# A graph layer with experts: an early expert order from seven token tiles, a list by matrix products, and maxima placed between attention units

## The chip, the core and the metric

The program runs on one core of a Trainium2 chip. The metric is device microseconds of one execution; of the kernel before, three runs gave a median of 1131.01 us (1125.94 to 1135.61). TensorE (PE) multiplies matrices into eight PSUM banks; VectorE (DVE), ScalarE (ACT) and GpSimd (POOL) compute; SyncE (SP) and POOL issue the DMAs. Each engine runs its own program in order, and they meet at semaphores.

## The reference

One layer on 1250 nodes of 768 channels, all float32. With `x` the input and `xn` its layer norm:

```
x = x + gnn(xn) + mix(xn)             # gnn holds its own norm, residual and Wu
gnn: out1 = gat(norm(xn), W1)  4 heads of 192;  out2 = gat(out1, W2)  2 heads of 96
     return concat(xn, out2) @ Wu + bu
gat: h = x @ W;  e = leaky_relu(s_src[src] + s_dst[dst], 0.2)
     ee = exp(e - max over the edges of dst);  out = sum(ee * h[src]) / sum(ee) + bias
mix: kqv = xn @ kqv_w.T + b;  linear attention over 12 heads with 32 features;  @ proj_w.T
x = x + ffn(layernorm(x))
ffn: probs = softmax(flat @ router_w.T)     # 8 experts
     top 2 of probs, each divided by 0.1 * sum of probs over all nodes + 0.91, then to sum 1
     out = sum over the two of gate * (silu(flat @ w1[e].T) @ w2[e].T)    # 768 -> 256 -> 768
```

The kernel turns the random edges into a dense table of counts, `cnt[src, dst]`.

## The kernel before

The nodes are ten **token tiles** (NT) of 128 rows, the last with 98. The five engine programs are written out by hand, and their order is the order of the work. PSUM banks are handed out in turn (`reserve`): `take` waits until the bank is free, `finished` until it is full, `evacuated` until it was copied.

**First half.** `x` is normalized and turned, keys, queries and mixing are multiplied in three-part float32 products, while VectorE and GpSimd build the table of counts. `u` (residual, mixture and the upper part of Wu) goes to `acc_d` in DRAM; `h1` is the product with W1 (20 steps, each half of a tile).

**Maxima.** For each destination tile, head and all sources, `masked_max` (L1337) subtracts a penalty (`pen`) from the row of scores (`a_row`) and takes the maximum. Tiles 0 to 3 are done for all heads at a time, then tiles 4 to 9 head by head. After each head `leaky_max` makes two columns, TensorE turns them (`mT`), VectorE copies them (L1375) and GpSimd writes them to `m_d` (L688). The rows `u1_row`, `u2_row` are read back broadcast to all partitions (L690, L695): head 0 behind the write of head 2, the others behind the last product of `h1`.

**Attention** (L1377, L991, L1896) goes through **units**: one head and one source tile. ScalarE makes `vbuf` (L1002), VectorE the score (`scores`, L1397), ScalarE the exponential (L1011), VectorE the product with `cnt` (L1408), TensorE ten matmuls (L1904) into five banks. There are three `pbuf` and two `vbuf`. The first attention has 40 units. Ahead of its first unit VectorE adds a bias row (L1451), and TensorE makes the small columns `b1T` (bias) and `csum` (sums of the router's columns), which VectorE takes behind the product of unit 0 (L1416 to L1420). Then come the product with W2, the same for two heads (`agg2`), and beside it products of `acc_d` with the router (`pre`).

**Routing.** When all `agg2` banks are copied (`rows_out_2`, L1438: five steps a bank), TensorE turns `o2` and multiplies each token tile with the lower part of Wu: two halves of 384 columns, and a separate pair of 8 columns for the router (`fin_step`, L1984). VectorE adds it to `x1` (`residual`, L1485), and SP stores `x1` into `out`. The tiles are routed in two `GROUPS`, 6 and 4: `shifted`, the softmax on ScalarE, `two_largest`; `ranks` on TensorE (prefix sums per expert, tile by tile) and `places` on VectorE. ScalarE normalizes `x1` into `yrow`, which SP stores into `y_d`, with the probabilities of the picks in its last 8 columns. GpSimd scatters each token's number to its place in `list_d` in DRAM (20 indirect DMAs, L724) and reads the list back. VectorE works out which expert each of the 27 **expert tiles** (NS) has, finds spare rows to fill the tiles (`matches`), and picks each tile's column out of the list (27 steps, L1612).

**Expert tiles.** For each, GpSimd fetches 128 rows of `y_d` (`fetch`, L733, three `xs` buffers), TensorE turns them, ScalarE and VectorE copy one half each into `xT` (L1111, L1645); then the first product (`first_product`, L2035), SiLU, a turn (`hT`), the second product, the gate, and GpSimd adds 128 rows into `out` by an indirect DMA (L751), each behind the end of the one before (L750).

## Time and profile before

| | |
|---|---|
| runs | 1131.01 us, median of 3 (1125.94 to 1135.61) |
| profiled execution | 1127.45 us; its span 1125.7 us |
| granted TensorE clock, mean | 0.905 |
| busy us: PE, PE's weight loads, DVE, ACT, POOL | 974.6, 831.3, 674.3, 417.4, 408.6 |
| first product of the first attention | starts 527.20 us |
| first fetch of an expert tile; first scatter | 922.21 us; 946.68 us |

### The profile page before, as it was taken

The page shows a single profiled execution, that of the slowest core. Times are in us where ns is not written, and L with a number is a line of the kernel's source. Part 1 is how long each engine was busy: PE and PEld are TensorE (multiplying, and loading weights), DVE is VectorE, ACT ScalarE, POOL GpSimd, SP SyncE. Part 2 cuts the span into 40 slices and gives each one's busy share as a digit, 9 for nine tenths or more (in the row PEclk, how much of TensorE's full clock was granted, in tenths as well). Part 3 has the DMA queues.
Part 4 walks back from the last instruction along what each step waited for, and adds up shares of the span by engine and source line. Part 5 has one row for each costly group of instructions (what it writes and reads, how often), then busy time and mean ns, then how long its engine had stood idle before and what let it go on. Part 6 is the DMA issues. An engine that isn't in the chain of part 4 may idle for free.

```text
span 1125.7 us, 14698 instructions
## 1 busy us (share of the span) xinstructions
PE 974.6 (87%) x5256; PEld 831.3 (74%) x5256; DVE 674.3 (60%) x1681; ACT 417.4 (37%) x658; POOL 408.6 (36%) x322
## 2 busy tenths in 40 slices
PE   3999988999999977964999989997789538999993
PEld 3898657776879977964999989896666436776772
DVE  7679997205643224678988868757957554333331
ACT  2544110333320003355788856438733302222220
POOL 3168888888888750003000000000000442344341
PEclk9999997899999988995999999868989558999997
DMA  9986456322544493114000000470054432656653
GB/s 294 220 202 161 78 114 168 62 24 1 113 65 76 84 266 132 25 43 177 13 15 1 1 1 1 154 269 13 1 177 173 138 129 50 133 115 121 129 119 56
DMA packets 77379, 115.77 MB, mean 103 GB/s; under 512 B 33089, under 2 KB 51899, under 8 KB 77309
## 3 DMA queue, kind: packets, MB, share of 16 engines
q0 software_dynamic: 36048, 40.48, 21.7%
q1 hardware_dynamic: 41261, 74.36, 20.4%
q8 instruction: 43, 0.70, 0.3%
q14 instruction: 27, 0.22, 0.1%
HBM read 85.18 MB, written 29.63 MB: 102 GB/s over the span
## 4 chain that ended last, share of the span: by engine, by line
PE 27%; DMA 15%; DVE 11%; issue 6%; ACT 3%; POOL 2%; another core or an unknown queue 1%; POOLq 0%; DVEq 0%; ACTq 0%
PE bank L1665 15%; DMA out<-yout,sb_negq 13%; PE bank L1904 9%; DVE pbuf L1408 3%; DVE pbuf L1397 3%; DVE sb_before L1342 2%; DMA cnt<-table 2%; PE bank L1676 1%; ACT h L988 1%; PE bank L1951 1%; ACT vbuf L1002 1%; POOL cnt L684 1%; DVE o L1443 1%; PE bank L1841 1%
## 5 line engine op out<-in xcount | busy, mean ns | idle before, releaser
L668 POOL DMA_INDIRECT table<-match_n,slot_ix x168 | 279.5, 1664 | 91.6 <-issue 47.2
L1904 PE MATMUL bank<-h,pbuf 128*128 128x193 f32 (+1 forms) x1200 | 189.8, 320 | 19.5 <-DVE pbuf L1408 18.9
L1904 PEld LDWEIGHTS bank<-h,pbuf 128*128 128x128 f32 x1200 | 182.9, 198 | 26.3 <-DVE pbuf L1408 23.7
L724 POOL DMA_INDIRECT list_d<-sb_wk,sb_negq x20 | 19.9, 993 | 331.9 <-DVE sb_negq L1561 326.4
L1342 DVE CUSTOM_DVE_ANT_0 sb_before<-a_row,pen 128x1280 bf16<-128x1280 f32 x60 | 89.4, 1491 | 18.7 <-ACT pen L945 12.5
L1206 DVE SCALAR_TENSOR_TENSOR junk_k<-keyrow,key,sb_before 128x384 uint8<-128x384 f32 x168 | 92.9, 615 | 9.1 <-DMA keyrow<-key_d 8.0
L1665 PE MATMUL bank<-xnT_hi,w_hi 128*128 128x512 f32 (+1 forms) x216 | 86.2, 399 | 10.6 <-issue 7.0
L1011 ACT ACTIVATE pbuf<-pbuf 128x1280 f32<-128x1280 f32 x60 | 76.7, 1278 | 42.4 <-DVE pbuf L1397 42.4
L1408 DVE SCALAR_TENSOR_TENSOR pbuf<-pbuf,cnt 128x1280 f32<-128x1280 f32 x60 | 88.8, 1487 | 0.0
L1665 PE MATMUL bank<-w_hi,xnT_hi 128*128 128x384 f32 x240 | 83.1, 346 | 0.0
L1665 PE MATMUL bank<-w_hi,xnT_lo 128*128 128x384 f32 x240 | 81.4, 339 | 0.0
L751 POOL DMA_INDIRECT out<-yout,sb_negq x27 | 42.9, 1589 | 105.8 <-DMA out<-yout,sb_negq 88.3
L1665 PE MATMUL bank<-w_lo,xnT_hi 128*128 128x384 f32 x240 | 81.3, 339 | 0.0
L1665 PE MATMUL bank<-w_all,xT 128*128 x324 | 76.8, 389 | 3.5 <-issue 3.5
L1665 PE MATMUL bank<-xnT_lo,w_hi 128*128 128x512 f32 (+1 forms) x216 | 79.4, 368 | 0.0
L1665 PE MATMUL bank<-xnT_hi,w_lo 128*128 128x512 f32 (+1 forms) x216 | 79.2, 366 | 0.0
L1665 PEld LDWEIGHTS bank<-w_all,xT 128*128 128x128 f32 x324 | 63.2, 196 | 18.3 <-issue 3.9
L1665 PE MATMUL bank<-w_all,hT 128*128 x216 | 74.8, 490 | 1.5 <-DVE hT L1652 1.5
L1397 DVE SCALAR_TENSOR_TENSOR pbuf<-u_row,sb_scol,vbuf 128x1280 f32<-128x1280 f32 x40 | 61.9, 1549 | 19.1 <-PE bank L1904 11.8
L833 ACT ACTIVATE kq<-bank,sb_kqb_c 128x512 f32<-128x512 f32 (+1 forms) x36 | 22.2, 618 | 123.3 <-PE bank L1665 103.2
L1665 PEld LDWEIGHTS bank<-xnT_hi,w_hi 128*128 128x128 f32 x216 | 42.2, 195 | 20.7 <-issue 14.5
L940 ACT ACTIVATE h<-bank,sb_rs 128x384 f32<-128x384 f32 x20 | 11.6, 582 | 122.3 <-PE bank L1665 122.3
(330 smaller groups left out, 1876.3 us busy)
## 6 DMA issues: line engine op xcount, KB each, us to landing
keyrow<-key_d SPq DMA_DIRECT2D x28, 384.0 KB
cnt<-table POOLq DMA_DIRECT2D x20, 320.0 KB, 8.9
w_all<-in_w1T SPq DMA_DIRECT2D x8, 768.0 KB
w_all<-in_w2T SPq DMA_DIRECT2D x8, 768.0 KB
u_row<-m_d POOLq DMA_DIRECT2D x8, 640.0 KB, 6.4
w_raw<-in_kqvT SPq DMA_DIRECT2D x4, 1152.0 KB, 16.9
y_d<-yrow SPq DMA_DIRECT2D x10, 388.0 KB
acc_d<-ubuf SPq DMA_DIRECT2D x20, 192.0 KB, 2.8
```

Source lines behind the costliest of these rows:

```text
L668: pool.indirect_dma_start(table[i], bass.IndirectOffsetOnAxis(ap=slot_ix[:, g:g + 1], axis=0), match_n[:, g:g + 1], None, compute_op=ALU.a ...
L724: pool.indirect_dma_start(list_d, bass.IndirectOffsetOnAxis(ap=place[0:n, k, t:t + 1], axis=0), token_no[0:n, t:t + 1], None, bounds_check ...
L751: pool.indirect_dma_start(out, bass.IndirectOffsetOnAxis(ap=sum_ix[:, s:s + 1], axis=0), yout[s % YO][:, :], None, compute_op=ALU.add, bou ...
L833: step(nc.scalar.activation(kq[j % 2][0][:, 0:w], b[:, 0:w], ACT.Identity, bias=kqb_c[:, col:col + 1]))
L940: nc.scalar.activation(h1[:, t, 2 * hf:2 * hf + 2, 0:C1], b[:, 0:HALF].rearrange("p (h c) -> p h c", h=2), ACT.Copy, scale=rs2[:, t:t + 1] ...
L1011: nc.scalar.activation(pbuf[i % 3][:, :], pbuf[i % 3][:, :], ACT.Exp).then_inc(e_done, 1)
L1206: nc.vector.scalar_tensor_tensor(out=junk_k[g % 2][:, :], in0=keyrow[c % KR][:, w:w + KW * P], scalar=key[:, g:g + 1], in1=before[:, first ...
L1342: ins = nc.vector.tensor_tensor_reduce(out=junk_m[:, :], in0=rows_a[h][:, :], in1=pen_t[:, :], scale=1.0, scalar=-3e38, op0=ALU.subtract, ...
L1397: nc.vector.scalar_tensor_tensor(out=pbuf[i % 3][:, :], in0=u1_r[h][:, :], scalar=scol[:, h, st:st + 1], in1=vbuf[i % 2][:, :], op0=ALU.ad ...
L1408: nc.vector.scalar_tensor_tensor(out=pbuf[i % 3][:, :], in0=pbuf[i % 3][:, :], scalar=2.0, in1=cnt[st][:, :], op0=ALU.min, op1=ALU.mult).t ...
L1665: return nc.tensor.matmul(o, l, r, start=first, stop=last)
L1904: ins = nc.tensor.matmul(b[:, d * stride:d * stride + chans + 1], score[:, dt * P:(dt + 1) * P], h_t[:, st, h, 0:chans + 1], start=st == 0 ...
```

## The change

**Expert order.** The groups are 7 and 3 tiles. From the first seven token tiles, which hold at least seven full expert tiles (NE), the first seven expert tiles are built and started: their rows are stored to a copy of their own (`early_d`) and fetched from there, while VectorE routes the last three. The other 20 wait for `y_d` and the late list. `x1` gets the 8 columns of probabilities and is normalized in place, after its store to `out`; `yrow` is gone, and there are four `xs`. For the early tiles ScalarE alone copies `xT`, `hT` and `y`.

**List.** The scatters to `list_d` are gone. For each pick two one-hot **marks** are made (row of the place; column times the token's number), and `listing` sums their products in a bank, 14 matmuls for the first group and 6 for the second, the latter between the first product of expert tile 2 and the turn of tile 1. `entries` picks the columns in two steps.

**Ranks and importance** are four and two matmuls wide in place of one or two for each tile. The router's 8 columns are merged into the first half of `wuo0` (392 columns), and `b2` is added by ScalarE when it copies `o2T`, so that `rows_out_2` has one product for five.

**Attention.** The maxima of heads 2 and 3 for tiles 4 to 9 stand behind twelve units of the first attention (`beside`), as do the bias row, the small columns and the rows of these heads. GpSimd writes heads 0 and 1 and reads their rows at once, before its table of numbers. ScalarE's ten steps on `cnt` (L975) stand in the last five tiles of `h1`. The core of the diff:

```diff
-        GROUPS = [range(6), range(6, NT)]
+        TABLE_W = E * KT
+        GA = 7
+        GROUPS = [range(GA), range(GA, NT)]
+        NE = -(-(2 * GA * P - E * (P - 1)) // P)
...
+                    r = slice(t * P, (t + 1) * P)
+                    if g == 0:
+                        sp.dma_start(early_d[r, :], x1[:, t, :]).then_inc(y_out[0], 16)
+                for t in tiles:
+                    r = slice(t * P, (t + 1) * P)
+                    sp.dma_start(y_d[r, :], x1[:, t, :]).then_inc(y_out[1], 16)
...
+
+            def rows_in_h(h):
                 pool.wait_ge(m_out[h], 16)
-            finished(pool, "h1", 1, NT - 1)
-            for h in range(1, H1):
                 pool.dma_start(u1_row[h][:, :], row_of(m_d, 2 * h)).then_inc(u_row_in[h], 16)
                 pool.dma_start(u2_row[h][:, :], row_of(m_d, 2 * h + 1)).then_inc(u_row_in[h], 16)
...
+            maxima_out(0), maxima_out(1)
+            finished(pool, "h1", 1, NT - 1)
+            rows_in_h(0), rows_in_h(1)
...
+            pool.wait_ge(y_out[0], 16 * GA)
             pool.wait_ge(rows_known, 1)
...
             for s in range(NS):
                 if s + XS < NS:
+                    if s + XS == NE:
+                        pool.wait_ge(y_out[1], 16 * NT)
+                        pool.wait_ge(rows_known, 2)
...
                 b = finished(act, "pen", dt, j)
                 nc.scalar.activation(pen[dt][:, 640 * j:640 * (j + 1)], b.bitcast(U16)[:, 0:640], ACT.Relu, scale=-BIG,
...
-                nc.scalar.activation(cnt[i][:, :], cnt[i][:, :], ACT.Identity, bias=less_c[:, 0:1]).then_inc(cnt_done, 1)
+                    if hf and t >= 5:
...
                 for t in GROUPS[g]:
-                    nc.scalar.activation(yrow[:, t, 0:D], x1[:, t, :], ACT.Identity, scale=rs2[:, t:t + 1],
+                    nc.scalar.activation(x1[:, t, 0:D], x1[:, t, 0:D], ACT.Identity, scale=rs2[:, t:t + 1],
                                          bias=shift[:, t:t + 1]).then_inc(y2_done, 1)
 
...
+                nc.vector.tensor_tensor(rw_raw[:, :, :], rw_raw[:, :, :], run[:, :].unsqueeze(1).broadcast_to([P, KD, E]),
+                                        ALU.add).then_inc(centred, 1)
+
+            beside = {3: (bias_row,), 6: (small_columns,), 9: (lambda: leaky_max_1(2),), 13: (lambda: maxima_rows(2),),
+                      21: (lambda: leaky_max_1(3),), 25: (lambda: maxima_rows(3),)}
+            for h, units in ((2, (1, 2, 4, 5, 7, 8)), (3, (10, 12, 14, 16, 18, 20))):
+                for dt, i in enumerate(units, 4):
+                    beside[i] = (lambda h=h, dt=dt: masked_max(pen[dt], a_row, (h,), dt),)
...
-                for d in range(5):
-                    ins = nc.vector.scalar_tensor_tensor(
-                        out=o2[:, 5 * i + d, h * C2:(h + 1) * C2], in0=pv[:, d, 0:C2], scalar=rec[:, d:d + 1],
-                        in1=b2_r[:, h * C2:(h + 1) * C2], op0=ALU.mult, op1=ALU.add)
-                    step(ins) if d < 4 else ins.then_inc(free("agg2", h, i), 1)
+                nc.vector.tensor_tensor(o2[:, 5 * i:5 * (i + 1), h * C2:(h + 1) * C2], pv[:, :, 0:C2],
+                                        rec[:, :].unsqueeze(2).broadcast_to([P, 5, C2]), ALU.mult).then_inc(free("agg2", h, i), 1)
...
+            def marks(g):
+
+                n = len(GROUPS[g])
+                for k in range(2):
+                    nc.vector.tensor_tensor(hot_row[:, k, 0:n, :], from_zero.unsqueeze(1).broadcast_to([P, n, P]),
+                                            chosen[g][:, k, 0, :].unsqueeze(2).broadcast_to([P, n, P]), ALU.is_equal)
+                    for i, t in enumerate(GROUPS[g]):
+                        ins = nc.vector.tensor_scalar(hot_col[:, k, i, :], columns, chosen[g][:, k, 1, i:i + 1],
+                                                      slot_no[:, t:t + 1], ALU.is_equal, ALU.mult)
+                    ins.then_inc(hot_done, 1)
...
+                hot = col_hot[:, 0:len(slots), :]
+                step(nc.vector.tensor_tensor(hot, columns.unsqueeze(1).broadcast_to([P, len(slots), TABLE_W]),
+                                             column[:, r].unsqueeze(2).broadcast_to([P, len(slots), TABLE_W]), ALU.is_equal))
...
+            def early_order():
+                step(nc.vector.tensor_tensor(filled[:, :, 0:NT - 1], n_early.unsqueeze(2).broadcast_to([P, E, NT - 1]),
+                                             steps_of.unsqueeze(1).broadcast_to([P, E, NT - 1]), ALU.is_ge))
+                step(nc.vector.tensor_reduce(out=n_full, in_=filled[:, :, 0:NT - 1], op=ALU.add, axis=AX.X))
+                tiles_before(n_full, first_early)
+                step(nc.vector.tensor_tensor(column_from, column_of, first_early, ALU.subtract))
+                in_order(EARLY_S, first_early, NE)
...
+            def entries(slots):
+                r, hot = slice(slots[0], slots[-1] + 1), col_hot[:, 0:len(slots), :]
+                step(nc.vector.tensor_tensor(hot, hot, listed.unsqueeze(1).broadcast_to([P, len(slots), TABLE_W]), ALU.mult))
+                step(nc.vector.tensor_reduce(out=row_f[:, r], in_=hot, op=ALU.add, axis=AX.X))
...
+            dve.wait_ge(pad_out, 16)
+            for t in GROUPS[0]:
+                residual(t)
+            inv_std_begin(mv3, span(0))
+            residual(GA)
+            shifted(0)
+            residual(GA + 1)
+            two_largest(0)
+            residual(GA + 2)
+            inv_std_begin(mv3, span(1))
+            places(0)
+            marks(0)
+            early_order()
+            b = finished(dve, "list", 0)
+            nc.vector.tensor_copy(listed, b[:, 0:TABLE_W]).then_inc(free("list", 0), 1)
+            evacuated(dve, "list", 0)
+            entries(EARLY_S)
+            nc.vector.tensor_scalar(token_ix[:, 0:NE], row_f[:, 0:NE], -1.0, None, ALU.add).then_inc(rows_known, 1)
+            shifted(1)
+            spare_places()
+            two_largest(1)
+            balances()
+            gates(0), gates(1)
+            places(1)
...
+            evacuated(dve, "spare")
+            marks(1)
+            gates(2), gates(3)
+            late_order()
+            b = finished(dve, "list", 1)
+            nc.vector.tensor_tensor(listed, listed, b[:, 0:TABLE_W], ALU.add).then_inc(free("list", 1), 1)
+            evacuated(dve, "list", 1)
+            entries(LATE_S)
+            r = slice(NE, NS)
...
-            b = take(pe, "csum")
-            for k in range(KD):
-                ins = mm(b[:, 0:E], ones[:, :], rw_raw[:, k, :], k == 0, k == KD - 1)
-            ins.then_inc(full("csum"), 1)
-            aggregate("agg", 0, H1, h1, S1, C1, 5, 2)
+                        if h * NT + st in behind:
+                            behind[h * NT + st]()
...
+            aggregate("agg", 0, H1, h1, S1, C1, 5, 2, {4: small_columns, 12: lambda: max_rows(2), 23: lambda: max_rows(3)})
...
-                        if hf == 0:
-                            evacuated(pe, "pre", len(PRE) - 1)
-                            for k in range(2):
-                                ins = mm(b[:, HALF:HALF + E], o2T[(t - 1) % 2][:, k, :], wuo_rw[:, k, :], k == 0, k == 1)
+                            w = wuo0[:, k, :] if hf == 0 else wuo[:, k, HALF:D]
+                            ins = mm(b[:, 0:w.shape[1]], o2T[(t - 1) % 2][:, k, :], w, k == 0, k == 1)
                         ins.then_inc(full("fin", t - 1, hf), 1)
...
+                of_group = slice(E * first, E * (first + n))
+                mm(b[:, 0:n * E], tri, row_t[:, 160:240][:, of_group], True, False)
+                mm(b[:, 0:n * E], ones[:, :], row_t[:, 240:320][:, of_group], False, True)
+                last = first + n - 1
+                mm(b[:, 64:64 + E], ones[:, :], seen[:, last, :], True, False)
+                mm(b[:, 64:64 + E], ones[0:rows(last), :], picks[0:rows(last), last, :], False, True).then_inc(full("rank", g), 1)
+
+            def listing(g):
+                b = take(pe, "list", g)
+                for k in range(2):
+                    pe.wait_ge(hot_done, 2 * g + k + 1)
+                    for i, t in enumerate(GROUPS[g]):
+                        n = rows(t)
+                        ins = mm(b[:, 0:TABLE_W], hot_row[0:n, k, i, :], hot_col[0:n, k, i, :], k == 0 and i == 0,
+                                 k == 1 and i == len(GROUPS[g]) - 1)
+                ins.then_inc(full("list", g), 1)
...
+            for t in range(NT + 1):
                 fin_step(t)
-            pe.wait_ge(numbers_done, 14)
+            pe.wait_ge(numbers_done, 12)
             ranks(0)
-            fin_step(NT)
-            ranks(1)
...
+                    if s + 1 == NE:
+                        pe.wait_ge(w_known, 2)
                     load_expert(s + 1)
                     first_product(s + 1)
+                if s == 0:
+                    spare_rows()
+                    ranks(1)
+                if s == 1:
+                    listing(1)
                 evacuated(pe, "h", s)
```

VectorE at the start of the first attention. Before:

```order
L1375 COPY sb_srow<-bank 20x128
L1451 TENSOR_TENSOR sb_row_b<-sb_row_b,sb_row_t 1x768
L1397 SCALAR_TENSOR_TENSOR pbuf_143<-u_row_133,sb_scol,vbuf_141 128x1280
L1397 SCALAR_TENSOR_TENSOR pbuf_144<-u_row_133,sb_scol,vbuf_142 128x1280
L1408 SCALAR_TENSOR_TENSOR pbuf_143<-pbuf_143,cnt_106 128x1280
L1416 COPY sb_b1T<-bank 96x8
L1418 TENSOR_SCALAR sb_run<-bank 128x8
L1420 TENSOR_TENSOR sb_rw_raw<-sb_rw_raw,sb_run 128x48
L1397 SCALAR_TENSOR_TENSOR pbuf_145<-u_row_133,sb_scol,vbuf_141 128x1280
L1408 SCALAR_TENSOR_TENSOR pbuf_144<-pbuf_144,cnt_107 128x1280
```

and now, where the names with `ISA` are a masked maximum and its read-out:

```order
L1405 COPY sb_srow<-bank 20x128
L1454 SCALAR_TENSOR_TENSOR pbuf_143<-u_row_133,sb_scol,vbuf_141 128x1280
L1454 SCALAR_TENSOR_TENSOR pbuf_144<-u_row_133,sb_scol,vbuf_142 128x1280
L1466 SCALAR_TENSOR_TENSOR pbuf_143<-pbuf_143,cnt_106 128x1280
L1454 SCALAR_TENSOR_TENSOR pbuf_145<-u_row_133,sb_scol,vbuf_141 128x1280
L1466 SCALAR_TENSOR_TENSOR pbuf_144<-pbuf_144,cnt_107 128x1280
L1374 ISA sb_before,sb_mxc<-a_row_119,pen_127 128x1280
L1374 ISA sb_mxc 128x1
L1454 SCALAR_TENSOR_TENSOR pbuf_143<-u_row_133,sb_scol,vbuf_142 128x1280
L1466 SCALAR_TENSOR_TENSOR pbuf_145<-pbuf_145,cnt_108 128x1280
```

The bias row is no longer ahead of the first score, the small columns are not behind the first product, and the first maximum of head 2 stands behind the product of unit 1.

TensorE between the last token tile and the first expert tile; `sb_row_t` with `sb_wq` or `sb_ones` are ranks, `sb_prob` the importance, `matches` the spare rows, `xs` the turned expert tiles. Before:

```order
L1665 MATMUL bank<-sb_row_t,sb_wq 128x8
L1665 MATMUL bank<-sb_row_t,sb_ones 128x8 x3
L1665 MATMUL bank<-sb_prob,sb_ones 128x8 x10
L1665 MATMUL bank<-sb_wq,matches 128x1 x8
L1676 MATMUL bank<-sb_ident,xs_171 128x128 x6
L1676 MATMUL bank<-sb_ident,xs_172 128x128 x6
L2045 TENSOR_LOAD sb_negq
L2045 ISA x2
L1665 ISA
```

and now, with the last token tiles at its head:

```order
L1770 MATMUL bank<-wuo,o2T_163 128x384 x2
L1770 MATMUL bank<-wuo_167,o2T_164 128x392 x2
L1770 MATMUL bank<-wuo,o2T_164 128x384 x2
L1770 MATMUL bank<-sb_row_t,sb_wq 128x56
L1770 MATMUL bank<-sb_row_t,sb_ones 128x56
L1770 MATMUL bank<-sb_row_t,sb_ones 128x8 x2
L1770 MATMUL bank<-hot_col,hot_row 128x80 x14
L1770 MATMUL bank<-sb_prob,sb_ones 128x72
L1770 MATMUL bank<-sb_prob,sb_ones 128x8
L2165 TENSOR_LOAD sb_negq
L2165 ISA x2
L1781 MATMUL bank<-sb_ident,xs_171 128x128 x6
L1781 MATMUL bank<-sb_ident,xs_172 128x128 x6
```

All token tiles are done before the ranks; those are four matmuls, the 14 list products follow, and the spare rows are gone from here. They stand with the ranks of the second group behind the first product of tile 1:

```order
L1770 MATMUL bank<-w_all,xT_181 128x256
L1770 MATMUL bank<-sb_wq,matches 128x1 x8
L1770 MATMUL bank<-sb_row_t,sb_wq 128x24
L1770 MATMUL bank<-sb_row_t,sb_ones 128x24
L1770 MATMUL bank<-sb_row_t,sb_ones 128x8 x2
L2186 MATMUL bank<-sb_ident,hs_176 128x128 x2
L1781 MATMUL bank<-sb_ident,xs_173 128x128 x6
```

so twelve small matmuls are new ahead of the turn (`hs`) of tile 0.

VectorE where the list comes in. Before, from the last step of the expert order:

```order
L1582 TENSOR_REDUCE sb_row_b<-sb_accb 128x27
L1597 CAST sb_negq<-sb_row_b 128x27
L1600 TENSOR_SCALAR matches<-sb_wq,sb_row_b 128x128 x8
L1604 TENSOR_SCALAR sb_run<-bank 128x8
L1606 TENSOR_SCALAR sb_run<-sb_run 128x8
L1607 RECIPROCAL sb_run<-sb_run 128x8
...
L1615 CAST sb_negq<-sb_row_t 128x3
L1612 SCALAR_TENSOR_TENSOR sb_row_b,sb_row_t<-sb_wq,sb_row_t,sb_negq 128x97 x24
L1615 CAST sb_negq<-sb_row_t 128x24
```

and now, for the first seven expert tiles:

```order
L1644 TENSOR_TENSOR col_hot<-sb_wq,sb_row_t 128x560
L1712 COPY sb_negq<-bank 128x80
L1670 TENSOR_TENSOR col_hot<-col_hot,sb_negq 128x560
L1671 TENSOR_REDUCE sb_row_t<-col_hot 128x7
L1715 TENSOR_SCALAR sb_negq<-sb_row_t 128x7
L1185 RECIPROCAL sb_rs<-sb_sq 128x3
L1186 TENSOR_TENSOR sb_r<-sb_rs 128x3
```

The 27 steps on the list are two large ones over seven tiles; the matches and the balances moved behind them.

## Rows read from the trace of the kernel before

**Rows 1.** The page: the chain that ended last, by line, share of the span.

```profile
PE bank L1665 15%; DMA out<-yout,sb_negq 13%; PE bank L1904 9%; DVE pbuf L1408 3%; DVE pbuf L1397 3%; DVE sb_before L1342 2%; DMA cnt<-table 2%; PE bank L1676 1%; ACT h L988 1%; PE bank L1951 1%; ACT vbuf L1002 1%; POOL cnt L684 1%; DVE o L
```

**Rows 2.** Timeline, VectorE, 493-522 us: start us, us, engine, line, operation, names, shapes, count.

```profile
493.70 1.49 DVE L1342 CUSTOM_DVE_ANT_0 sb_before<-a_row,pen 128x1280 bf16<-128x1280 f32 x1
...
495.24 1.49 DVE L1342 CUSTOM_DVE_ANT_0 sb_before<-a_row,pen 128x1280 bf16<-128x1280 f32 x1
...
520.97 0.94 DVE L1451 TENSOR_TENSOR sb_row_b<-sb_row_b,sb_row_t 1x768 f32<-1x768 f32 x1
```

**Rows 3.** Timeline, GpSimd and ScalarE, 500-520 us; in brackets the idle time before, and its releaser.

```profile
500.30 0.53 POOL L688 DMA_DIRECT2D m_d<-sb_srow  x1 [10.24 <-DVE sb_srow L1375]
...
511.42 0.55 POOL L690 DMA_DIRECT2D u_row<-m_d  x1
...
517.37 2.61 ACT L1002 ACTIVATE vbuf<-u_row,sb_a 128x1280 f32<-128x1280 f32 x2 [5.99 <-DMA u_row<-m_d]
```

**Rows 4.** DMA issues, 496 to 535 us: count, KB each, median us to landing.

```profile
w2g_raw<-in_W SPq DMA_DIRECT2D x1, 576.0 KB, 5.1
```

**Rows 5.** Timeline, TensorE, 517-533 us; and one row of the chain, us of six units.

```profile
527.20 6.05 PE L1904 MATMUL bank<-h,pbuf 128*128 128x193 f32 x20
...
608.71 19.98 PE bank L1904 x120
```

**Rows 6.** Timeline, VectorE, 572-576 us: first two units back to back.

```profile
572.63 1.48 DVE L1408 SCALAR_TENSOR_TENSOR pbuf<-pbuf,cnt 128x1280 f32<-128x1280 f32 x1
...
575.49 1.48 DVE L1408 SCALAR_TENSOR_TENSOR pbuf<-pbuf,cnt 128x1280 f32<-128x1280 f32 x1
```

**Rows 7.** Windows of 4 us: length, busy us by engine, granted clock, DMA share, GB/s.

```profile
796.00:800.00 4.00, 3.22 (x27) 2.89 (x26) 4.00 (x4) 3.66 (x4) 0.00 (x0) 1.00 0.00 0
...
812.00:816.00 4.00, 2.16 (x12) 1.92 (x12) 3.95 (x4) 2.05 (x2) 0.00 (x0) 0.53 0.00 0
...
896.00:900.00 4.00, 3.31 (x16) 3.32 (x16) 0.53 (x4) 0.00 (x0) 3.08 (x4) 0.50 1.03 381
```

**Rows 8.** Timeline, TensorE, 836-943 us.

```profile
836.22 1.06 PE L1676 MATMUL bank<-sb_ident,o 128*96 128x128 f32 x4 [3.14 <-DVE o L1443]
...
849.71 0.51 PE L1665 MATMUL bank<-sb_row_b,o2T 96*128 96x8 f32 x4
...
850.07 1.54 PE L1665 MATMUL bank<-wuo,o2T 96*128 96x384 f32 x4
...
853.32 1.54 PE L1665 MATMUL bank<-wuo,o2T 96*128 96x384 f32 x4
...
876.01 0.57 PE L1665 MATMUL bank<-sb_row_t,sb_wq 128*128 128x8 f32 x2 [4.91 <-issue]
...
876.43 0.57 PE L1665 MATMUL bank<-sb_row_t,sb_ones 128*128 128x8 f32 x2
...
933.40 7.97 PE L1665 MATMUL bank<-w_all,xT 128*128 x24 [3.51 <-issue]
```

**Rows 9.** Timeline, VectorE, 870-934 us.

```profile
870.98 0.20 DVE L1512 TENSOR_REDUCE sb_r<-sb_prob 128x6 f32<-128x48 f32 x1
...
881.31 0.17 DVE L1546 TENSOR_SCALAR sb_row_b<-sb_row_t 128x8 f32<-128x8 f32 x1 [5.40 <-PE bank L1665]
...
881.78 0.61 DVE L1549 TENSOR_TENSOR sb_accb<-bank,sb_wq 128x432 f32<-128x432 f32 x1
...
920.03 0.32 DVE L1612 SCALAR_TENSOR_TENSOR sb_row_b<-sb_wq,sb_row_t,sb_negq 128x97 f32<-128x97 f32 x1 [8.25 <-DMA sb_negq<-list_d]
...
932.65 1.02 DVE L1645 COPY xT<-bank 128x384 f32<-128x384 f32 x2
```

**Rows 10.** Timeline, GpSimd, 922-1117 us.

```profile
922.21 1.06 POOL L734 DMA_INDIRECT xs<-y_d,sb_negq  x1 [3.80 <-DVE sb_negq L1615]
...
946.68 1.65 POOL L751 DMA_INDIRECT out<-yout,sb_negq  x1 [9.77 <-DVE yout L1659]
...
1115.49 1.55 POOL L751 DMA_INDIRECT out<-yout,sb_negq  x1 [4.67 <-DMA out<-yout,sb_negq]
```

470 lines of the change are left out of this document (245 added, 225 removed).

## The prediction

> **What bounds the kernel now.** I read the chain of waits first, then the windows, then the timeline of each engine at the places that the change touches. By line the chain is matrix products of the first half (15%), the scatters into `out` (13%) and the attention products (9%) [rows 1]. Three stretches matter.
>
> *Before and in the first attention.* VectorE makes the masked maxima at 1.54 us each [rows 2], six a head for four heads, until 520.8; TensorE stands still. The u rows of head 0 are fetched only behind the maxima of head 2: issued at 511.42, used by ScalarE at 517.37, so 5.95 us [rows 3]. TensorE begins at 527.20, at half clock (6.05 us for the first unit), and then takes 19.98 / 6 = 3.33 us a unit [rows 5]. VectorE needs 575.49 - 572.63 = 2.86 us a unit [rows 6]: TensorE bounds, and VectorE has 0.47 us to spare in each unit.
>
> *Routing.* The second attention's products end 3.14 us before 836.22, at 833.1; the restart runs at half clock, then a token tile takes 853.32 - 850.07 = 3.25 us [rows 8]. VectorE then routes in two groups, waits 5.40 us for the first ranks and 8.25 us for the list that goes through DRAM [rows 9]; the first token rows are fetched at 922.21 and the first scatter starts at 946.68 [rows 10].
>
> *Expert tiles.* 27 scatters, each behind the one before: (1115.49 - 946.68) / 26 = 6.49 us [rows 10]. The end is the first scatter plus a fixed 26 x 6.49.
>
> **The attention.** The u rows of head 0 can now be asked for right behind the maxima of head 1, at 500.30 + 0.6 = 500.9 [rows 3]; they would be there at 506.9, but share the DMA engines with the load of W2, which takes 5.1 us to land [rows 4], and that of Wu. Bounds: 506.9 (no sharing) and 506.9 + 5.1 = 512.0 (all of it); I take 508.5, nearer to the first, since those loads start earlier. Leak 1.3 (half of 2.61 [rows 3]), two scores of 1.5 and a product of 1.4 (a pair is 2.86 [rows 6]) put the first matmul at 514.2, 13.0 us earlier than 527.20. The bias row (0.94 [rows 2]) and the 5 us of small columns between VectorE and TensorE are no longer ahead of it; they go behind units 3 to 6.
>
> But VectorE now carries twelve maxima in units 1 to 20. Until product 20 is made: 20 pairs x 2.86 = 57.2, 12 x 1.54 = 18.5, bias row, small columns, one leaky maximum and one row copy 2.7; so 514.2 + 78.4 = 592.6, plus 3.33 for its matmuls: 595.9. Before, TensorE had unit 20 done at 527.20 + 6.05 + 20 x 3.33 = 599.9. A head's change costs both about 1.4 by ScalarE's bank copies, and some 1.5 more where VectorE is the one that is late; the second leaky maximum adds 0.8. Left: 4.0 - 2.3 = 1.7; I take **-1 us**. The gain is lost since VectorE, which has the rows of head 1 copied by 500.3 [rows 3], stands idle until the u rows are there, and pays the maxima later, when it has 0.47 us a unit to hide them. Bounds: -4 and +5 (landing at its two ends, and the waits at the heads' change doubled).
>
> The move of ten subtractions on ScalarE into the last tiles of h1 costs nothing: they are hidden by the h1 products, and done by 502, before the u rows; uncovered they would hold product 0 (12 us in one piece before). Head 2's rows are ready by unit 17 and needed at 19.
>
> **Routing, as a table of times** (profile's clock, attention left out):
> - Second attention's end: one product of 480 elements in place of five steps, and TensorE asks for the first bank alone. Transposes start at 833.1 instead of 836.2: -3.1. Without the idle 3.14 us the clock should stay at its upper level (I assume it).
> - A token tile: 3.25 less 850.07 - 849.71 = 0.36 for the eight-column matmuls [rows 8], plus 0.03: 2.9. Ten tiles in a row: 834.3 + 29 = 863.3; the seventh at 854.6, its sums and statistics on VectorE 2 us later, 856.6.
> - A residual is two sums and two statistics passes over 384 elements, 0.5 each by the 0.61 for 432, and two small steps of 0.2: 2.5. The top two of six tiles took from 870.98 to 881.31 - 5.40 = 875.9, so 5.5 for seven [rows 9]. Residual 7 with one step more, shifts (nine small steps), residual 8, top two: 2.7 + 1.9 + 2.5 + 5.5, so 869.2. Ranks are four matmuls in place of twelve; one takes 876.43 - 876.01 = 0.43 us at half clock [rows 8], done at 871.1, hidden by residual 9 (2.5 us, to 871.7). The wait of 5.40 is gone.
> - Places: two steps of 504 elements at 0.7 (by 0.61 for 432) and ten small ones of 0.23: 3.7. Marks: per pick 896 elements, by the same row 1.1 us (bounds 0.9 and 1.3), and seven of 80 elements at some 0.18 (0.17 for 8, 0.32 for 97 [rows 9]): 2 x 2.3 = 4.6. Order of seven tiles: some 16 small steps of 0.2 to 0.3 and one of 560 elements: 4.2. To 884.2. The 14 list matmuls (0.43 each, 6 us) overlap with the last two and are done at 884. List, entries, indices: 0.3 + 2 x 0.75 + 0.2: **886.1**.
> - Stores: two weight loads (1.57 MB) and seven tiles (2.78 MB) from 871.5 at 381 GB/s [rows 7] are 11.4 us: 883 to 884, so no wait, if they are served in order.
> - Fetch at 886.3 against 922.21: **-35.9**.
> - Fetch to scatter: 24.5 us before. The 3.51 us idle ahead of the first product [rows 8], which ended when VectorE, busy with the list until then, had copied xT at 932.65 + 1.02 [rows 9], is gone, since ScalarE copies: -3.5. The fetch flies beside the second copies of the stores: +1.5 (0 to +5). Twelve small matmuls (spare rows, ranks of group 1) now stand before the first hT: 2.7 at full clock, 5.2 at half: +2.7. The second half of y is copied behind the first: +0.6. Gates: shifts, matches, top two, balances and two gates (some 10 us of small steps) end about 896, ahead of the first y at 909.7. Sum +1.3, taken down to +0.7 for the longer cover of the evacuations.
> - First scatter: 946.7 - 35.9 + 0.7 = **911.5**, -35.2.
> - Six list matmuls between first products cost tile 1 some 1.3; TensorE has about 0.3 a tile to spare: **+1**.
> - Late list: VectorE waits for ranks at 905.7, then places 2, marks 2.1, gates 2, order 6.5, entries 2 x 1.75 and rest: 923.5. GpSimd wants it behind scatter 2, at 925; TensorE needs those rows at 936. Hidden; if late beyond some 8 us, each us counts.
>
> Sum against the profiled execution: 1127.45 - 35.2 + 1 - 1 = 1092.3. The median shown, 1131.01, is 3.6 above it; I take about half of that: **1094 us**.
>
> At one point a rule speaks against the change. In the windows VectorE paces TensorE at 796 to 800 with 3.22 of 4 us busy, and the clock is full; at 812 to 816 with 2.16 busy it is 0.53 [rows 7]. In the new attention TensorE would be busy 3.33 of 4.4 us, so 3.0 of 4, between the two. The Trainium skill (TensorE: Matmul & The Clock Gate, "A second HAM failure mode: psum-queue depth-cycling") says that frequent short idle times between groups of matmuls can make the clock swing. By the row the sum is the one above; by that rule it is rival C.
>
> **Rivals.**
> - A, the first fetch is held by the stores. If the second copies (2.78 MB more) are served with the first ones, all seven land at 871.5 + 7.13 MB / 381 GB/s = 890.2 instead of 884, 4 us behind the list, and the fetch may take 4 more: 1102. For it: the DMA share is 1.03 while such stores run [rows 7]. The Trainium skill (DMA: Bandwidth & Descriptors, "Issuing engines are not separate DMA queues") says that issues of different engines interleave on the same engines, which is this rival's ground. Against: the stores stand in one queue in the right order.
> - B, VectorE's attention stretch is longer: waits of the kind at the heads' change recur in each unit with a maximum, 0.8 us x 12: 1104.
> - C, slower: half clock through units 0 to 25. A unit then takes 6.05: 514.2 + 26 x 6.05 = 671.5 against 527.2 + 6.05 + 25 x 3.33 + 1.4 = 617.9, +54 in place of -1: 1149. It decides only if 17 or more of 26 units run so, as 2.72 a unit has to eat 34 us and 11 more. Against it: at half clock a unit fills VectorE's 4.4 us wholly, TensorE has no idle left, and it came back from such a state in the first attention within two units.
> - D, the early tiles start no earlier than some 895 and B holds as well, or C for a third of the units: 1120, within 1%.
>
> **How the numbers follow.** Forecast 0.68, A 0.14, B 0.10, C 0.04, D 0.04. Its own range is 1087 to 1101 by the bounds above. To leave out C and D and little else the range is 1084 to 1111. A measurement here can tell about 1%, 11 us: faster 0.92, same 0.04, slower 0.04.
>
> **What would show it.** Right: first matmul of the first attention near 514, its last about where it was; transposes at 833 with a full clock; first fetch near 886, first scatter near 911, 6.5 us steps, no wait of TensorE for tile 7. Wrong: a u row used after 512; granted clock under 0.9 in units 1 to 20; the fetch released by a store; a gap ahead of scatter 7.

## The result, and the profile after

The changed kernel takes 1093.36 us, the median of four runs (1085.47 to 1098.63), against 1131.63 us (1125.94 to 1135.61) of the kernel before: a ratio of 0.967, 95% interval 0.963 to 0.971. Two later comparisons gave 0.971 (0.967 to 0.975) and 0.965 (0.962 to 0.969). The profiled execution took 1085.47 us, span 1083.7, granted clock 0.933: it is the fastest of the four, 6.8 us under the sum of the forecast, while the median lies 1 us above that sum.

The page's chain by line, as [rows 1] (L1770 and L2008 are the helpers' lines that were L1665 and L1904):

```profile
PE bank L1770 15%; DMA out<-yout,sb_negq 13%; PE bank L2008 6%; DVE pbuf L1466 5%; DVE pbuf L1454 4%; DMA cnt<-table 3%; PE bank L1781 1%; ACT vbuf L1025 1%; DMA early_d<-x 1%; ACT h L1011 1%; DVE sb_before L1374 1%; PE bank L2061 1%; DMA u_row<-m_d 1%; DMA xs<-early_d,sb_negq 1%; POOL cnt L707 1%
```

The scatters' share is the 13% that it was. New in the chain is `early_d<-x`, the stores of the early tiles.

**First attention.** VectorE, start and length, as [rows 2]: its copy of head 1's rows, the first scores, and two of head 3's maxima behind units.

```profile
502.38 0.28 DVE L1405 COPY sb_srow<-bank 20x128 f32<-20x128 f32 x1 [0.37 <-PE bank L1937]
...
512.95 3.01 DVE L1454 SCALAR_TENSOR_TENSOR pbuf<-u_row,sb_scol,vbuf 128x1280 f32<-128x1280 f32 x2 [10.28 <-ACT vbuf L1025]
...
575.52 1.47 DVE L1374 CUSTOM_DVE_ANT_0 sb_before<-a_row,pen 128x1280 bf16<-128x1280 f32 x1
...
582.66 1.47 DVE L1374 CUSTOM_DVE_ANT_0 sb_before<-a_row,pen 128x1280 bf16<-128x1280 f32 x1
```

TensorE in the same places, as [rows 5]:

```profile
517.41 12.48 PE L2008 MATMUL bank<-h,pbuf 128*128 128x193 f32 x60 [15.07 <-DVE pbuf L1466]
...
572.60 6.80 PE L2008 MATMUL bank<-h,pbuf 128*128 128x193 f32 x40 [0.63 <-DVE pbuf L1466]
...
579.92 6.80 PE L2008 MATMUL bank<-h,pbuf 128*128 128x193 f32 x40 [0.52 <-DVE pbuf L1466]
```

The first product comes 15.0 us behind the copy of head 1's rows (27.7 before). The first u rows are used at 511.47, 9.1 us behind that copy. From 575.52 on VectorE repeats every 7.14 us (582.66 - 575.52): two units of 2.86 and a masked maximum. TensorE stands idle 0.52 to 0.63 us ahead of each such pair and is no longer the bound. One window over this stretch shows what the clock did (columns as in [rows 7]):

```profile
530.00:610.00 80.00, 72.30 (x433) 68.07 (x433) 75.67 (x85) 56.20 (x61) 1.66 (x3) 1.00 0.05 18
```

TensorE busy 72.30 of 80 us, clock 1.00 throughout.

**Second attention.** VectorE's copies of two finished banks stand between units; the first of them, before (five steps), and the wait for TensorE that follows:

```profile
805.74 1.73 DVE L1443 SCALAR_TENSOR_TENSOR o<-bank,sb_rec,sb_accb 128x96 f32<-128x96 f32 x5
...
819.64 1.55 DVE L1397 SCALAR_TENSOR_TENSOR pbuf<-u_row_b,sb_scol,vbuf 128x1280 f32<-128x1280 f32 x1 [1.46 <-PE bank L1904]
```

and after (one step), with a window over the stretch that follows it:

```profile
802.26 0.66 DVE L1494 TENSOR_TENSOR o<-bank,sb_rec 128x480 f32<-128x480 f32 x1
```

```profile
804.00:808.00 4.00, 2.69 (x24) 2.52 (x24) 3.93 (x5) 2.75 (x3) 0.00 (x0) 1.00 0.00 0
```

From 796 to 820, cut in windows of 4 us, this is the least that TensorE is busy in the changed kernel (2.69 of 4), and the clock is 1.00 in all of them. Before, it was busy 1.61 of 4 us at 808 to 812, and the clock of the next window is 0.53 [rows 7].

**Routing.** TensorE, as [rows 8]:

```profile
825.82 0.61 PE L1781 MATMUL bank<-sb_ident,o 128*96 128x128 f32 x4
...
826.92 2.88 PE L1770 MATMUL bank<-wuo,o2T 96*128 96x392 f32 x8 [0.49 <-ACT o2T L1103]
...
829.85 2.77 PE L1770 MATMUL bank<-wuo,o2T 96*128 96x392 f32 x8
...
861.38 0.65 PE L1770 MATMUL bank<-sb_row_t,sb_wq 128*128 128x56 f32 x2 [6.16 <-issue]
...
886.77 2.82 PE L1781 MATMUL bank<-sb_ident,xs 128*128 128x128 f32 x12 [2.95 <-DMA xs<-early_d,sb_negq]
```

The first transposes overlap the last products of the attention (3.14 us idle before); a token tile takes 829.85 - 826.92 = 2.93 and then 2.83 us. The ranks begin at 861.38 and are eight records in place of 24. VectorE, as [rows 9], in the first group: ranks read, places, a mark of 896 elements, and the row numbers handed to GpSimd:

```profile
863.82 0.17 DVE L1590 COPY sb_row_b<-bank 128x8 f32<-128x8 f32 x1
...
864.70 0.68 DVE L1596 TENSOR_TENSOR sb_accb<-bank,sb_wq 128x504 f32<-128x504 f32 x1
...
867.47 1.09 DVE L1613 TENSOR_TENSOR hot_row<-sb_wq,sb_row_b 128x896 f32<-128x896 f32 x1
...
878.52 0.17 DVE L1715 TENSOR_SCALAR sb_negq<-sb_row_t 128x7 uint32<-128x7 f32 x1
```

The rank row has no idle time in brackets: the wait of 5.40 us is gone. The last row ends the early list at 878.7. GpSimd, as [rows 10]: first fetch, scatters 0 and 1, the fetch of tile 7 (the first from `y_d`), last scatter:

```profile
879.71 1.13 POOL L747 DMA_INDIRECT xs<-early_d,sb_negq  x1 [244.63 <-DMA early_d<-x]
...
904.79 1.64 POOL L771 DMA_INDIRECT out<-yout,sb_negq  x1 [14.54 <-DVE sb_row_b L1695]
...
912.22 2.39 POOL L771 DMA_INDIRECT out<-yout,sb_negq  x1 [4.40 <-ACT yout L1160]
...
921.12 1.06 POOL L747 DMA_INDIRECT xs<-y_d,sb_negq  x1 [0.30 <-issue]
...
1074.50 1.56 POOL L771 DMA_INDIRECT out<-yout,sb_negq  x1 [4.75 <-DMA out<-yout,sb_negq]
```

The first fetch names an early store as its releaser, but it starts 1.0 us behind the end of the list, and in the repeat a0 below, where the list is named, it is 0.95: the stores ended at about the time of the list. TensorE uses the fetched rows at 886.77, 7.06 us after the issue. Before it was 4.03, from 922.21 [rows 10] to this row:

```profile
926.24 1.54 PE L1676 MATMUL bank<-sb_ident,xs 128*128 128x128 f32 x6 [11.34 <-DMA xs<-y_d,sb_negq]
```

The fetch of tile 7 had no wait.

Here is the way from one profiled execution to the other, cut at events that both have:

| stretch | before | after | difference | forecast |
|---|---|---|---|---|
| start to the copy of head 1's rows | 499.46 | 502.38 | +2.9 | 0 |
| to the last product of the first attention | 167.03 | 165.52 | -1.5 | -1 |
| to the first product of the second | 102.87 | 97.97 | -4.9 | 0 |
| to its last product | 63.73 | 60.04 | -3.7 | 0 |
| to the first transposes | 3.13 | -0.09 | -3.2 | -3.1 |
| to the first fetch | 85.99 | 53.89 | -32.1 | -32.8 |
| to the first scatter | 24.47 | 25.08 | +0.6 | +0.7 |
| to the last scatter | 168.81 | 169.71 | +0.9 | +1 |
| to the end | 10.21 | 9.20 | -1.0 | 0 |
| sum | | | -42.0 | -35.2 |

### The profile page after: what moved, and what is told of

Its sections match the earlier page's. It is cut to its first block, busy times and chain, and to the rows that moved or that the text cites. A ratio compares the mean times of both kernels' runs of the same rounds, so it can differ in the third digit from the quotient of the medians.

```text
span 1083.7 us, 14577 instructions
## 1 busy us (share of the span) xinstructions
PE 947.0 (87%) x5216; PEld 809.1 (75%) x5216; DVE 667.2 (62%) x1635; ACT 427.8 (39%) x689; POOL 386.6 (36%) x298
## 4 chain that ended last, share of the span: by engine, by line
PE 23%; DMA 18%; DVE 12%; issue 6%; ACT 3%; POOL 1%; SPq 0%; POOLq 0%; DVEq 0%; ACTq 0%
PE bank L1770 15%; DMA out<-yout,sb_negq 13%; PE bank L2008 6%; DVE pbuf L1466 5%; DVE pbuf L1454 4%; DMA cnt<-table 3%; PE bank L1781 1%; ACT vbuf L1025 1%; DMA early_d<-x 1%; ACT h L1011 1%; DVE sb_before L1374 1%; PE bank L2061 1%; DMA u_row<-m_d 1%; DMA xs<-early_d,sb_negq 1%; POOL cnt L707 1%
## 5 line engine op out<-in xcount | busy, mean ns | idle before, releaser
L2008 PE MATMUL bank<-h,pbuf 128*128 128x193 f32 (+1 forms) x1200 | 189.9, 318 | 38.8 <-DVE pbuf L1466 35.8
L2008 PEld LDWEIGHTS bank<-h,pbuf 128*128 128x128 f32 x1200 | 180.7, 195 | 47.7 <-DVE pbuf L1466 43.4
L747 POOL DMA_INDIRECT xs<-early_d,sb_negq x7 | 7.4, 1058 | 250.5 <-DMA early_d<-x 244.6
L1770 PE MATMUL bank<-xnT_hi,w_hi 128*128 128x512 f32 (+1 forms) x216 | 85.4, 395 | 12.6 <-issue 9.0
L1770 PE MATMUL bank<-w_hi,xnT_hi 128*128 128x384 f32 x240 | 83.9, 350 | 0.0
L1770 PE MATMUL bank<-w_hi,xnT_lo 128*128 128x384 f32 x240 | 82.3, 343 | 0.0
L1770 PE MATMUL bank<-w_lo,xnT_hi 128*128 128x384 f32 x240 | 82.1, 342 | 0.0
L1770 PE MATMUL bank<-xnT_lo,w_hi 128*128 128x512 f32 (+1 forms) x216 | 78.8, 365 | 0.0
L1770 PE MATMUL bank<-xnT_hi,w_lo 128*128 128x512 f32 (+1 forms) x216 | 78.3, 363 | 0.0
L1770 PE MATMUL bank<-w_all,hT 128*128 x216 | 76.7, 498 | 1.5 <-DVE hT L1755 1.5
L1770 PE MATMUL bank<-w_all,xT 128*128 x324 | 74.9, 382 | 0.0
L1770 PEld LDWEIGHTS bank<-w_all,xT 128*128 128x128 f32 x324 | 62.1, 192 | 13.9
L1770 PEld LDWEIGHTS bank<-w_all,hT 128*128 128x128 f32 x216 | 39.2, 191 | 27.3 <-issue 3.3
L1770 PEld LDWEIGHTS bank<-xnT_hi,w_hi 128*128 128x128 f32 x216 | 41.8, 193 | 22.5 <-issue 16.5
```

The lines of the kernel that those rows point to most:

```text
L1770: return nc.tensor.matmul(o, l, r, start=first, stop=last)
L2008: ins = nc.tensor.matmul(b[:, d * stride:d * stride + chans + 1], score[:, dt * P:(dt + 1) * P], h_t[:, st, h, 0:chans + 1], start=st == 0 ...
```

## Experiments

All changes are to the changed kernel, and all ratios are to the kernel before, measured beside it. Two runs repeat the changed kernel as a base. Times of one kernel spread by up to 1.5%, so most verdicts rest on stretches of the trace, each from one profiled execution.

**The changed kernel again.**

> The changed kernel again, as the base of the others. Theory T1 (the forecast's working held; the profiled execution came 6.8 us below the sum because TensorE's clock was granted fully in two stretches that the change does not touch): ratio to the kernel before 0.965 to 0.969, and in this profile the first fetch comes 53 to 55 us after the end of the second attention's products, the first scatter 25 us after the fetch, the other 26 scatters 6.5 us apart, while the time from the first attention's last product to the second's last is anywhere between 158 and 167 us. Rival T2 (the change itself shortened that middle stretch): it is 158 us again, within 1 us.

Ratio 0.9711 (0.9673 to 0.9749), a little above the range expected. From transposes to fetch 53.83 us, fetch to scatter 24.84, the other 26 scatters 6.66 apart and not 6.5: 173.1 us from the first to the last, where the kernel before took 168.8 and the first profile of the changed one 169.7. In the twelve profiles of the changed kernel and its variants it is 169.7 to 173.1; of the kernel before there is one. The middle stretch, from the last product of the first attention to the last of the second, took 162.9: T2 falls, but T1 holds in half only. Cut in two, the second attention is 60.04 us here too, as in all profiles of kernels with the one-step copy, so that part belongs to the change. The stretch between the attentions is what varies. The same 656 to 658 products, in the kernel before, in the changed one, and in e9 below, one window each:

```profile
666.49:769.36 102.87, 90.43 (x658) 89.45 (x657) 68.39 (x215) 52.71 (x153) 0.00 (x0) 0.81 0.36 120
```

```profile
667.90:765.87 97.97, 85.54 (x656) 84.56 (x656) 68.36 (x215) 52.48 (x153) 0.00 (x0) 0.85 0.38 129
```

```profile
658.49:767.81 109.32, 96.88 (x658) 95.83 (x657) 68.37 (x215) 52.91 (x153) 0.00 (x0) 0.76 0.35 115
```

Their length goes with the granted clock: 0.81, 0.85, 0.76 for 102.87, 97.97, 109.32 us. In this repeat it was 102.87, as in the kernel before.

> The changed kernel once more, beside e10_fill_hold on the same chip: ratio to the kernel before 0.966 to 0.971. In its profile the second attention takes 60.0 us, and from the end of its products to the first fetch 53.8, as in the two before; the stretch between the attentions takes anything from 98 to 109 us, in steps that go with half clock.

Ratio 0.9652 (0.9618 to 0.9686), just below the range expected. Second attention 60.04, then 53.99 from the transposes to the first fetch, the stretch between the attentions 101.24; the first and the last scatter 172.8 apart.

**The maxima ahead of the attention.**

```diff
-            beside = {3: (bias_row,), 6: (small_columns,), 9: (lambda: leaky_max_1(2),), 13: (lambda: maxima_rows(2),),
-                      21: (lambda: leaky_max_1(3),), 25: (lambda: maxima_rows(3),)}
-            for h, units in ((2, (1, 2, 4, 5, 7, 8)), (3, (10, 12, 14, 16, 18, 20))):
-                for dt, i in enumerate(units, 4):
-                    beside[i] = (lambda h=h, dt=dt: masked_max(pen[dt], a_row, (h,), dt),)
+            beside = {3: (bias_row,), 6: (small_columns,), 13: (lambda: maxima_rows(2),), 25: (lambda: maxima_rows(3),)}
+            for h in (2, 3):
+                for dt in range(4, NT):
+                    masked_max(pen[dt], a_row, (h,), dt)
+                leaky_max_1(h)
```

> All twelve maxima of heads 2 and 3 stand ahead of the first attention again, where VectorE waits for the u rows; everything else as changed. T1 (placing them beside the units was worth about nothing, since the gain ahead is paid back in the units): the first product starts near 527 instead of 517, units take 3.33 us each, the last product ends 667 +- 2 as with the change; time within 0.3% of the changed kernel. Rival T3 (the placement carries part of the gain): the last product ends 8 to 13 us later and the time is 0.7 to 1.2% above the changed kernel.

The last product came at 672.99, with head 1's rows copied at 502.05: 170.9 us between them, against 165.5, 166.8 and 165.5 in the three profiles of the changed kernel. So 4 to 5 us worse, between T1 and T3. TensorE at the start, and a window over the stretch where the last two rows begin:

```profile
526.64 15.83 PE L2008 MATMUL bank<-h,pbuf 128*128 128x193 f32 x80 [24.63 <-DVE pbuf L1466]
...
546.12 1.51 PE L1770 MATMUL bank<-sb_ones,sb_row_b 1*96 1x1 f32 x16
...
547.90 2.02 PE L1770 MATMUL bank<-sb_rw_raw,sb_ones 128*128 128x8 f32 x12
...
549.78 30.04 PE L2008 MATMUL bank<-h,pbuf 128*128 128x193 f32 x160
```

```profile
547.00:560.00 13.00, 13.00 (x69) 12.91 (x69) 6.16 (x8) 4.78 (x4) 0.00 (x0) 0.74 0.00 0
```

TensorE bounds the units here, and the small columns between units 4 and 5 take 3.7 us of it (3.2 in the changed kernel). Behind them eight units take 30.04 us and not 8 x 3.33 = 26.6, since the clock of 547 to 560 is 0.74: 3.4 us. Such a stretch need not belong to the edit. Behind the same small columns, e10 below ran 540 to 550 at a clock of 0.66 and e2, with the same attention code, at 1.00. Without these 3.4 us e1 would stand at 167.5, 1 to 2 us above the changed kernel, which T1 allows. So the run speaks against T3; it doesn't show that the placement beside the units is worth anything. In time this kernel was at 0.9648 (0.9603 to 0.9693), no slower than the changed one measured beside it (0.9711), with intervals that overlap.

**Maxima of head 2 in the wait for the u rows.**

```diff
-            beside = {3: (bias_row,), 6: (small_columns,), 9: (lambda: leaky_max_1(2),), 13: (lambda: maxima_rows(2),),
+            beside = {3: (bias_row,), 6: (small_columns,), 13: (lambda: maxima_rows(2),),
                       21: (lambda: leaky_max_1(3),), 25: (lambda: maxima_rows(3),)}
-            for h, units in ((2, (1, 2, 4, 5, 7, 8)), (3, (10, 12, 14, 16, 18, 20))):
-                for dt, i in enumerate(units, 4):
-                    beside[i] = (lambda h=h, dt=dt: masked_max(pen[dt], a_row, (h,), dt),)
+            for dt in range(4, NT):
+                masked_max(pen[dt], a_row, (2,), dt)
+            leaky_max_1(2)
+            for dt, i in enumerate((1, 5, 8, 12, 15, 19), 4):
+                beside[i] = (lambda dt=dt: masked_max(pen[dt], a_row, (3,), dt),)
```

> Six maxima of head 2 stand in the 10.3 us in which VectorE waits for the u rows; those of head 3 stand behind units 1, 5, 8, 12, 15 and 19. T1: VectorE's 0.47 us to spare in a unit then hides one maximum in three to four units, TensorE bounds all units: start at 517, 6.0 + 39 x 3.33 + 3 x 1.4 = 140, so the last product ends at 657 to 660 instead of 667.9, and the time is 8 to 10 us (0.7 to 0.9%) below the changed kernel. Rival T4 (the units are paced by waits of the three score buffers, not by VectorE's sum): at most 2 us are gained.

Ratio 0.9604 (0.9574 to 0.9633), 1.0% under the changed kernel measured beside it, so 11 us, of which the attention in the trace shows 5 to 6.5. Start of the products to their end 144.9 us, so 160.25 from the copy of head 1's rows, 5.2 to 6.5 less than with the change. T4 falls. T1's 140 was too short: it left out the small columns (3.2 us), and each maximum still costs TensorE a pause:

```profile
552.69 13.67 PE L2010 MATMUL bank<-h,pbuf 128*128 128x193 f32 x80 [0.74 <-DVE pbuf L1468]
...
567.11 10.12 PE L2010 MATMUL bank<-h,pbuf 128*128 128x193 f32 x60 [0.63 <-DVE pbuf L1468]
...
577.97 13.38 PE L2010 MATMUL bank<-h,pbuf 128*128 128x193 f32 x80 [0.74 <-DVE pbuf L1468]
...
592.09 10.80 PE L2010 MATMUL bank<-h,pbuf 128*128 128x193 f32 x60 [0.74 <-DVE pbuf L1468]
```

0.63 to 0.74 us stand ahead of each restart. In the group of four units from 577.97 to 592.09 VectorE's sum is the smaller one (4 x 2.86 + 1.49 = 12.93 against 4 x 3.33 = 13.32), and the pause is there all the same.

**Bias row and small columns in that wait too.**

```diff
-            beside = {3: (bias_row,), 6: (small_columns,), 9: (lambda: leaky_max_1(2),), 13: (lambda: maxima_rows(2),),
+            beside = {2: (lambda: masked_max(pen[9], a_row, (2,), 9), lambda: leaky_max_1(2)), 13: (lambda: maxima_rows(2),),
...
+            bias_row()
+            for dt in range(4, NT - 1):
+                masked_max(pen[dt], a_row, (2,), dt)
+            small_columns()
+            for dt, i in enumerate((5, 8, 11, 14, 17, 20), 4):
+                beside[i] = (lambda dt=dt: masked_max(pen[dt], a_row, (3,), dt),)
...
-            aggregate("agg", 0, H1, h1, S1, C1, 5, 2, {4: small_columns, 12: lambda: max_rows(2), 23: lambda: max_rows(3)})
+            small_columns()
+            aggregate("agg", 0, H1, h1, S1, C1, 5, 2, {12: lambda: max_rows(2), 23: lambda: max_rows(3)})
```

> As e2_fill, and the bias row and the small columns stand ahead of the first attention too, in the wait for the u rows; the sixth maximum of head 2 stands behind unit 2 and those of head 3 behind units 5, 8, 11, 14, 17 and 20. T1 (TensorE bounds the units once VectorE's maxima are hidden, so what it does between units counts in full): the 3.5 us of small columns between units 4 and 5 are gone, and from VectorE's copy of head 1's rows to the last product of the attention it takes 156 to 157.5 us, where e2_fill took 160.25 and the changed kernel 165.5 to 166.8. Rival T8 (the small columns ahead push the first product later by as much): 160 us again.

160.21 us, as T8 said, but not for its reason: the first product came no later (15.29 us behind the copy). The columns were done by 502.4, and then:

```profile
499.62 2.73 PE L1773 MATMUL bank<-sb_rw_raw,sb_ones 128*128 128x8 f32 x12
...
510.53 11.64 PE L2011 MATMUL bank<-h,pbuf 128*128 128x193 f32 x60 [8.17 <-DVE pbuf L1469]
...
523.73 10.11 PE L2011 MATMUL bank<-h,pbuf 128*128 128x193 f32 x60 [1.56 <-DVE pbuf L1469]
...
534.59 10.12 PE L2011 MATMUL bank<-h,pbuf 128*128 128x193 f32 x60 [0.74 <-DVE pbuf L1469]
```

With a maximum in every third unit, three units take 10.86 us, while TensorE's sum is 9.99 and VectorE's 10.07 (3 x 2.86 + 1.49): the pauses (1.56, then 0.74 each), now seven maxima beside units and not six, ate what the columns gave back. Ratio 0.962 (0.959 to 0.966).

**Five steps for a bank of the second attention.**

```diff
-                nc.vector.tensor_tensor(o2[:, 5 * i:5 * (i + 1), h * C2:(h + 1) * C2], pv[:, :, 0:C2],
-                                        rec[:, :].unsqueeze(2).broadcast_to([P, 5, C2]), ALU.mult).then_inc(free("agg2", h, i), 1)
+                for d in range(5):
+                    ins = nc.vector.scalar_tensor_tensor(
+                        out=o2[:, 5 * i + d, h * C2:(h + 1) * C2], in0=pv[:, d, 0:C2], scalar=rec[:, d:d + 1],
+                        in1=ones[:, 0:C2], op0=ALU.mult, op1=ALU.mult)
+                    step(ins) if d < 4 else ins.then_inc(free("agg2", h, i), 1)
```

> The copy of each bank of the second attention is five steps of VectorE again (0.35 us each, the multiplier of ones in the place of b2) instead of one of 0.66 us. Theory T6 (a term the forecast left out: two of the four copies stand between units of the second attention, which VectorE bounds, and the longer ones leave TensorE idle until its clock is halved): from the first to the last product of the second attention 63.7 us instead of 60.04, and 1 us more ahead of the transposes behind it; 4 to 5 us in all. Rival T7 (the copies beside units cost only their own length): 60.04 + 2 x 1.07 = 62.2, and 1 more behind, so 3.2 us in all.

The second attention took 64.64 us and 0.98 more until the transposes: 5.7 us in all, T6's mechanism at a somewhat larger size; T7's 62.2 falls. Of the 4.6 us within the attention about 2.1 are the longer copies themselves (2 x 1.07). VectorE, and then two windows over the same place (columns as in [rows 7]):

```profile
811.82 1.73 DVE L1495 SCALAR_TENSOR_TENSOR o<-bank,sb_rec,sb_ones 128x96 f32<-128x96 f32 x5
...
826.08 1.55 DVE L1454 SCALAR_TENSOR_TENSOR pbuf<-u_row_b,sb_scol,vbuf 128x1280 f32<-128x1280 f32 x1 [1.81 <-PE bank L2011]
```

```profile
812.00:818.00 6.00, 3.61 (x32) 3.45 (x32) 5.68 (x12) 4.31 (x4) 0.00 (x0) 1.00 0.00 0
...
818.00:824.00 6.00, 4.32 (x22) 4.08 (x22) 5.93 (x6) 3.63 (x3) 0.00 (x0) 0.51 0.00 0
```

TensorE is busy 3.61 of 6 us while VectorE makes the steps, the granted clock falls to 0.51 in the next window, and only then VectorE waits for TensorE (1.81 us). With the one-step copy, in the changed kernel above, neither happens. The ratio was 0.9669 (0.9627 to 0.9711); 5 us are 0.5%, which the times here don't resolve.

**No early start.**

```diff
-            pool.wait_ge(rows_known, 1)
+            pool.wait_ge(rows_known, 2)
             for s in range(XS):
                 fetch(s)
```

with `spare_rows`, `ranks(1)` and `listing(1)` ahead of the first turned tile and the gates behind the late list. The early tiles are still fetched from `early_d`, not from `y_d` as the expectation has it; it is the late list that they wait for.

> The first seven expert tiles wait for the late list and for y_d, as all tiles did before; list by products, merged ranks and the rest as changed. The order on VectorE is: early list, routing of the last three tiles, late list, then the gates. T1: late list at 878.7 + 1.9 + 1.7 + 4 + 1 + 3 + 2.3 + 5 + 5.6 = 903, first fetch there instead of 879.7, first scatter near 925 instead of 904.8, so 19 to 21 us above the changed kernel, and 14 to 16 us of the 35 at the tail come from the list, the ranks and the earlier transposes. Rival T5 (the early start only moves the wait into the expert tiles): under 8 us above.

Ratio 0.983 (0.979 to 0.987), 14 us above the changed kernel measured beside it. GpSimd's first fetch and first scatter:

```profile
911.39 1.14 POOL L744 DMA_INDIRECT xs<-early_d,sb_negq  x1 [278.61 <-DVE sb_negq L1728]
...
931.97 1.64 POOL L768 DMA_INDIRECT out<-yout,sb_negq  x1 [12.92 <-ACT yout L1157]
```

From the transposes to the fetch 79.7 us instead of 53.8, from the fetch to the scatter 20.6 instead of 24.8, and 6.50 instead of 7.42 to the next scatter. Net 20.7 us of the trace, as T1 said (19 to 21), though the median times differ by 14 only; T5 (under 8) falls. Of the 31.5 that the change takes between transposes and first scatter, the early start is 21.6, and 10 are the list without DRAM, the merged ranks and what goes with them. No run takes the list alone back to DRAM, so its own share isn't shown.

**Ranks tile by tile.**

```diff
-                mm(b[:, 0:n * E], tri, row_t[:, 160:240][:, of_group], True, False)
-                mm(b[:, 0:n * E], ones[:, :], row_t[:, 240:320][:, of_group], False, True)
+                for i in range(n):
+                    one = slice(E * (first + i), E * (first + i + 1))
+                    mm(b[:, i * E:(i + 1) * E], tri, row_t[:, 160:240][:, one], True, False)
+                    mm(b[:, i * E:(i + 1) * E], ones[:, :], row_t[:, 240:320][:, one], False, True)
```

> The ranks are matrix products tile by tile again (two for each token tile and two for the sums: 16 in place of 4 for the first group). T1 (the wait of 5.40 us for the ranks went because four products end within the residual of one tile): 16 x 0.43 = 6.9 us behind the top two, so VectorE waits 4.3 to 5 us again ahead of the places of the first group and the first fetch comes that much later, 58 to 59 us behind the second attention instead of 53.8. Rival T9 (the wait was due to something else, such as the clock of TensorE after its pause): under 2 us.

VectorE waits again, and the first fetch comes 58.39 us behind the transposes instead of 53.8 to 54.0:

```profile
876.03 0.17 DVE L1590 COPY sb_row_b<-bank 128x8 f32<-128x8 f32 x1 [4.48 <-PE bank L1770]
```

T1 holds, T9 falls: some 4.5 of those 10 us are the merged ranks. One time was taken, 1099.63 us.

**Stores held behind the fetches.**

```diff
+                if g == 0:
+                    sp.wait_ge(xs_in[1], 16)
                 for t in tiles:
                     r = slice(t * P, (t + 1) * P)
                     sp.dma_start(y_d[r, :], x1[:, t, :]).then_inc(y_out[1], 16)
```

> The stores of the first seven tiles into y_d wait until the second fetch has landed. Rival A of the forecast, the part that the profile bears out (fetches share the DMA engines with these stores): the first two fetches are used 4 to 4.5 us after the first is issued instead of 7, the first scatter comes 22.5 us behind the first fetch instead of 25, and nothing waits for y_d later. If the fetches take 7 us for another reason (four of them in flight), they still do.

GpSimd's fetch and scatter, and TensorE's first use of it:

```profile
880.41 1.13 POOL L749 DMA_INDIRECT xs<-early_d,sb_negq  x1 [247.83 <-DVE sb_negq L1717]
...
901.22 1.64 POOL L773 DMA_INDIRECT out<-yout,sb_negq  x1 [10.85 <-ACT yout L1162]
```

```profile
884.51 1.54 PE L1783 MATMUL bank<-sb_ident,xs 128*128 128x128 f32 x6
```

The fetch is used 4.10 us after its issue, not 7, with the same four fetches in flight: the stores were what held it. The first scatter comes after 20.8 us, not 25, which is more than that. The profiles, cut at the first use of the rows, show where the rest is (e5 has another order of work there and is left out):

| | stores into `y_d` | fetch to its use | use to first scatter | clock there |
|---|---|---|---|---|
| changed, a0, a1, e2 | beside the fetch | 7.06, 6.75, 6.95, 6.79 | 18.02, 18.09, 17.98, 17.98 | 0.79 |
| e7 | beside the fetch | 6.73 | 18.63 | 0.77 |
| e1, e8 | beside the fetch | 7.07, 6.78 | 16.31, 16.06 | 0.89, 0.90 |
| e6 | nearly done | 4.07 | 21.81 | 0.71 |
| e4, e10 | held | 4.10, 4.20 | 16.71, 16.64 | 0.89 |
| e9 | held | 4.07 | 19.84 | 0.74 |

So the stores cost about 3 us of landing. The part behind it goes with the granted clock, 16 to 22 us, and e1 and e8 have the short one without held stores. One time was taken, 1084.98 us; a single one proves nothing at this spread.

**Together.** e9 has e8's edits, the held stores, and

```diff
-            load_w2(0), load_w2(1)
             for g, tiles in enumerate(GROUPS):
...
                         sp.dma_start(early_d[r, :], x1[:, t, :]).then_inc(y_out[0], 16)
+                if g == 0:
+                    load_w2(0), load_w2(1)
```

> e8_columns with the held stores, and the last two loads of expert weights behind the early stores. If all theories hold: attention 8 to 10 us shorter than with the change, first fetch 1 us earlier and first scatter 3 to 4 us earlier on top, so 11 to 13 us below the changed kernel: a ratio to the kernel before of 0.956 to 0.960. If the loads held the first product instead (they now land at about 880, and TensorE wants them at 886), that last part is lost.

Ratio 0.9606 (0.9572 to 0.964), just above the range expected. The attention took 160.5 us from the copy of head 1's rows, 5 to 6 less than with the change and not 8 to 10, and the first fetch came 53.84 us behind the transposes, where it is in the changed kernel too, and not 1 us earlier. The moved loads did not hold the first product. The fetch was used after 4.07 us, yet the scatter came 23.9 us after it, for the clock: the same 8 us of e4 and of e9, one window each:

```profile
886.00:894.00 8.00, 7.51 (x39) 6.78 (x38) 2.70 (x21) 3.52 (x6) 1.01 (x1) 0.86 0.98 353
```

```profile
886.00:894.00 8.00, 7.50 (x27) 6.16 (x26) 3.71 (x26) 3.63 (x6) 1.76 (x2) 0.59 0.98 353
```

> e2_fill (six maxima of head 2 in the wait for the u rows, those of head 3 spread) with the stores into y_d held until the second fetch has landed. From the two profiles: 5 to 6.5 us shorter from VectorE's copy of head 1's rows to the last product of the first attention, and 2 to 4 us shorter from the first fetch to the first scatter than with the change; 8 to 10 us in all, a ratio to the kernel before 0.7 to 0.9% under that of the changed kernel in the same call. If a held store delays the late tiles, a gap stands ahead of scatter 7 and the gain is lost.

Ratio 0.9609 (0.9578 to 0.9639) beside 0.9652 of the changed kernel: 0.45% less, not 0.7 to 0.9. Fetch to scatter 20.84 as hoped, no gap at scatter 7, but the attention took 164.0 from the copy of head 1's rows where the same code took 160.25 in e2: TensorE ran at 0.68 and 0.64 of its clock in the two halves of 540 to 550, where e2 had 1.00. So e2, e8, e9 and e10 all lie below both kernels, at 0.960 to 0.962, and can't be ranked among themselves. Only e2's interval is clear of that of a changed kernel measured beside it; e10's overlaps it (0.9618 to 0.9686), and e8 and e9 had no changed kernel beside them.

## Why the prediction was right

- **Routing and the first fetch** (-3.1 and -32.8): -3.2 and -32.1. The table of times was off by 0.7 us over 53; ranks, marks, order and list took what the rows said. The e6 run shows the mechanism of the ranks and e5 that of the early start; the list without DRAM has no run of its own. The late list was there 35.8 us behind the first fetch (915.5), forecast 37.2, and hidden.
- **Fetch to scatter** (+0.7): +0.6, with a larger part on each side. The fetch landed 3.0 us later and not 1.5, by e4 because of the stores; this is the ground of rival A. Its price (8 us) was far too high, since the early stores had ended by about the time of the list. The rest of the stretch took 2.4 us less (18.02 against 20.44) and not 0.8, at a granted clock of 0.79 against 0.70; so that the two cancel is partly luck.
- **The serial scatters** (+1): +0.9 in the first profile, all of it between scatters 0 and 1 (7.43 us), as forecast; in e5, which has no list products there, it is 6.50. But the repeats have +4.3 and +4.0, with the same 7.42 and 7.43 there and the rest spread over later scatters. So the fixed 26 x 6.49 was too low by some 3 us for the changed kernel as it usually ran. Whether the change slows them, or the one profile of the kernel before was a quick one, stays open.
- **The first attention** (-1): -1.5, and -0.3 and -1.6 in the repeats. The u rows were used 9.1 us behind the copy of head 1's rows, forecast 9.0 (508.5 against 499.46). The sign of being wrong, a use after 512, held in the profile (511.47) and not in the repeats (513.35, 513.01), where all that stands ahead came later. The gain ahead (12.7 us) is paid back, as forecast, because VectorE stands idle 10.28 us ahead of the scores and bounds the units afterwards; e2 shows that it is this idle time. By e1, where the maxima stand, ahead or beside, made little difference, as the forecast has it.
- **Rival C** (half clock through units) did not occur: clock 1.00 with TensorE busy 72.30 of 80 us. The rule on frequent short idle times, which the Trainium skill gives (TensorE: Matmul & The Clock Gate, "A second HAM failure mode: psum-queue depth-cycling"), is not borne out in this stretch; in e7, with TensorE busy 3.61 of 6 us, the clock of the next 6 us was 0.51, as it says. Rival B did not occur either: VectorE repeats a pair of units and a maximum every 7.14 us, with no wait in it. (The pauses of 0.74 in e2 and e8 are TensorE's, another thing of a similar size.)
- **The step that was missing** is the second attention. I priced the shorter bank copy only at its end (-3.1) and took the rest as unchanged. Two of the four copies stand between units that VectorE bounds, and the longer ones took TensorE to half clock: another -3.7; e7, which takes the steps back, loses 4.6. The window of 812 to 816 in [rows 7] was that very place; I read it as evidence on a rule and not as a cost that the change removes.
- **Luck** is the rest of the 6.8 us between sum and profiled time: +2.9 ahead of the first attention, -4.9 between the attentions and -1.0 at the end. The edits leave TensorE's work in the first two as it was; the copy of head 1's rows came anywhere from 495.2 to 504.9 in the twelve profiles of the changed kernel and its variants. Their median is 502.2, and the kernel before has one profile, 499.46, so a small cost of ScalarE's moved steps isn't excluded. The median, 1093.4, is 0.6 us from the forecast partly because of such terms, not only because the sum was right.

## What to carry to other kernels

When one engine's work is moved beside another's, look at both ends: the place it leaves (is the engine idle there, waiting for a transfer?) and the place it goes to (which engine bounds it?). Here work paid best in the wait (e2), and only what didn't fit belonged beside the units. A step that is made shorter in a helper is shorter wherever the helper is called: list all its calls, and look at each for the clock behind it. And cut two traces at common events before explaining a difference, since stretches that no edit touches can differ by more than the edit is worth. Before a term is called confirmed, look at it in the repeats too: the scatters agreed with the forecast in one profile of three.

## What the runs showed of the hardware

- The same 656 to 658 products between the attentions took 98.0 to 109.3 us over 13 profiles, with a granted clock of 0.85 to 0.76. TensorE is busy 87 to 89% of that stretch; what decides the level there stays open.
- The first of several indirect fetches of 128 rows was used 4.0 to 4.2 us after its issue where the stores were held or all but done (six profiles), and 6.7 to 7.1 us beside plain stores of 388 KB each (seven).
- From the first use of those rows to the first scatter the changed kernel and its variants took 16.1 us at a granted clock of 0.90 and 21.8 at 0.71.
- In an attention with three score buffers a masked maximum of 1.49 us behind a unit costs TensorE 0.74 us (e2, e8), in a group of four units even with VectorE's sum below TensorE's (12.93 against 13.32 us).
